# Cross attention and top-2 experts on one core: the norms' last step on ACT, shared weight loads for the scores, one bias product, keys by batch, half of the weight splits on GpSimd

## What is computed

```python
def xattn(query, kv, Wq, bq, Wkv, bkv, Wo, bo):      # 16 heads of 16
    q = query @ Wq + bq
    k, v = split(kv @ Wkv + bkv)
    bias = -slopes[:, None, None] * abs(arange(Nk)[None] - arange(Nq)[:, None] - (Nk - Nq))
    scores = einsum("bhqd,bhkd->bhqk", q, k) / sqrt(16) + bias
    return (softmax(scores) @ v) @ Wo + bo
def ffn(x, Wg, bg, W1, b1, W2, b2):                  # 8 experts, hidden 1024
    gate = softmax(x @ Wg + bg); s, idx = top_k(gate, 2); s = s / (sum(s) + 1e-8)
    return sum over the two chosen e of s_e * (gelu(x @ W1[e] + b1[e]) @ W2[e] + b2[e])
x = x + xattn(layernorm(x), ctx_1024, ...)
x = x + ffn(layernorm(x), ...)
```

## Time and profile before

| | us |
|---|---|
| median of 3 runs | 503.34 |
| lowest, highest | 501.44, 504.68 |
| profiled execution | 508.91 |
| its span | 507.1 |
| busy in the span: PE, DVE, ACT, POOL | 419.6, 312.6, 232.4, 223.7 |
| mean granted clock of PE | 0.922 |

### The profile page before, as it was taken

One profiled execution on the slowest core, in us unless ns is written; L12 is line 12 of the kernel. 1 busy time (PEld: TensorE's weight loads), 2 busy tenths in 40 slices (PEclk: granted clock), 3 DMA queues, 4 the chain that ended last, 5 costly groups with the idle time before them and its releaser, 6 DMA issues. The chain is left out here.

```text
span 507.1 us, 16158 instructions
## 1 busy us (share of the span) xinstructions
PE 419.6 (83%) x5137; PEld 330.3 (65%) x5138; DVE 312.6 (62%) x875; ACT 232.4 (46%) x607; POOL 223.7 (44%) x305
## 2 busy tenths in 40 slices
PE   5565768897888999995179899989989998999981
PEld 2554556676666778873168677668867876777760
DVE  5357848796778777554526466636664765566560
ACT  1333636564555564563234444534543553445430
POOL 3123528887888886677602222222222232122232
PEclk9865979898989999998579999989998999999997
DMA  6574455555646535333322223113222322122110
GB/s 225 134 229 150 139 152 189 175 175 192 215 136 185 165 123 163 122 123 127 127 64 37 39 41 53 35 29 45 46 44 31 53 38 43 34 43 47 22 12 0
DMA packets 52967, 50.70 MB, mean 100 GB/s; under 512 B 22672, under 2 KB 47024, under 8 KB 52784
## 3 DMA queue, kind: packets, MB, share of 16 engines
q1 hardware_dynamic: 45192, 41.07, 27.0%
q0 software_dynamic: 7152, 8.47, 9.9%
q10 hardware_dynamic: 576, 0.53, 0.3%
HBM read 33.73 MB, written 17.50 MB: 101 GB/s over the span
## 5 line engine op out<-in xcount | busy, mean ns | idle before, releaser
L976 PE MATMUL ps<-area,wts 128*128 128x128 f16 (+1 forms) x2896 | 197.0, 243 | 0.1
L976 PEld LDWEIGHTS ps<-area,wts 128*128 (+1 forms) x2896 | 157.5, 103 | 41.0 <-issue 2.1
L976 PE MATMUL ps<-wts,area 128*128 x624 | 153.4, 330 | 2.2 <-DVE area L934 1.8
L718 ACT ACTIVATE area<-ps,late 128x128 f32<-128x128 f32 x312 | 89.2, 368 | 115.0 <-PE ps L976 115.0
L932 DVE TENSOR_SCALAR area<-area 128x512 f16<-128x512 f32 x78 | 33.0, 424 | 77.8 <-ACT area L718 77.7
L976 PE MATMUL ps<-area 128*128 128x154 f16 (+2 forms) x928 | 71.0, 236 | 12.0 <-DMA area<-qd 11.1
L976 PEld LDWEIGHTS ps<-area 128*128 128x128 f16 (+1 forms) x928 | 59.8, 107 | 21.2 <-issue 8.1
L595 POOL DMA_INDIRECT out<-o,row_id x20 | 31.6, 1579 | 95.1 <-issue 65.0
L595 POOL DMA_INDIRECT out<-xn,row_id x19 | 30.0, 1579 | 92.4 <-issue 79.8
L804 DVE TENSOR_REDUCE mx<-ps 128x3 f32<-128x462 f32 (+1 forms) x96 | 53.1, 579 | 24.3 <-PE ps L976 23.9
L621 ACT ACTIVATE area<-ps 128x512 f32<-128x512 f32 x80 | 47.3, 595 | 27.7 <-PE ps L976 25.5
(11 more groups left out here) (121 smaller groups left out, 419.1 us busy)
## 6 DMA issues: line engine op xcount, KB each, us to landing
stage<-in_w SPq DMA_DIRECT2D x32, 512.0 KB, 5.0
area<-xlist SPq DMA_DIRECT2D x39, 130.0 KB, 2.0
area<-qd SPq DMA_DIRECT2D x16, 256.0 KB, 2.7
qd<-wts SPq DMA_DIRECT2D x48, 64.0 KB, 1.9
area<-in_x SPq DMA_DIRECT2D x16, 128.0 KB, 2.3
out<-area SPq DMA_DIRECT2D x16, 128.0 KB, 1.8
xlist<-pad_rows SPq DMA_DIRECT2D x11, 130.0 KB, 2.5
area<-in_b SPq DMA_DIRECT2D x1, 1024.0 KB, 5.0
```

The costliest lines, as they stand in the source:

```text
L718: last = nc.scalar.activation(h32[par][:, c * P:(c + 1) * P], h_ps[par][m][:, f * P:(f + 1) * P], ACT.Gelu_apprx_tanh, bias=b1T[:, ds(e * ...
L976: return nc.tensor.matmul(out_, lhsT, rhs, start=start, stop=stop, skip_group_check=skip)
```

## The change

- `normed1` and `normed2` on POOL end with an operation on one column (-mean x rstd, `rs[:, 2]`); the step on 128x256 is an ACT activation with scale and bias read per partition. ACT has that of the second norm first in its turn, and that of the first norm behind exponential 4 (in the first turns behind the query copy).
- Of a turn's two weight units, the second: ACT makes the high half, then scales the staged unit in place (a third pass), and POOL subtracts, one turn later, between the gate weights and the second norm's `pow`. DVE keeps the first unit.
- Scores: heads go in pairs that share one query weight; one product of 314 columns covers both where both lie in one group. Six of sixteen loads and products go away.
- The output bias is one product of two rows instead of two products of one.
- Keys, their splits and their writes to memory are made batch by batch; ACT issues the writes of the bias rows. In turns before 0 the query product stands ahead of the scores, and DVE's `norm1` ahead of its maxima.

```diff
-GROUPS = [(0, 3), (3, 3), (6, 3), (9, 3), (12, 2), (14, 2)]
+GROUPS = [(0, 3), (3, 3), (6, 2), (8, 3), (11, 3), (14, 2)]
 # SP
+            sp.dma_start(a_sb[:, 0:A_ONE], pack_a[:, 0:A_ONE]).then_inc(s.a_in0, 16)
             load_x(0)
-            sp.dma_start(a_sb, pack_a).then_inc(s.a_in, 16)
...
+            for b in range(B):
+                sp.wait_ge(s.k_hi, b + 1)
+                for a in (0, 1):
+                    sp.dma_start(parts[:, a, :, b], k16[:, b, 0]).then_inc(S[f"kd_w{b}"], 16)
+                sp.wait_ge(s.k_lo, b + 1)
+                sp.dma_start(parts[:, 2, :, b], k16[:, b, 1]).then_inc(S[f"kd_w{b}"], 16)
+                if b == 0:
+                    write_q(0)
 # POOL
+            def rstd(t, mv, rs, ready, done, shifted):
+                pool.wait_ge(ready, t + 1)
                 pool.tensor_tensor(rs[:, 1:2], rs[:, 0:1], c32[:, C_HALF:C_HALF + 1], ALU.pow).then_inc(done, 1)
+                pool.wait_ge(done, t + 1)
+                pool.tensor_scalar(rs[:, 2:3], mv[:, 0:1], rs[:, 1:2], -1.0, ALU.mult, ALU.mult).then_inc(shifted, 1)
-                pool.tensor_scalar(xn, xr[:, t % 8, :], mv1[:, 0:1], rs1[:, 1:2], ALU.subtract, ALU.mult).then_inc(s.xn_d, 1)
...
+            def split_w_lo(u):
+                pool.wait_ge(s.w_sc, seconds.index(u) + 1)
+                pool.tensor_tensor(unit_place(u, 1), staged(u), unit_place(u, 0), ALU.subtract).then_inc(S[f"w_lo{u % NSTAGE}"], 1)
...
                 if f1 is not None:
-                    normed1(f1)
+                    rstd(f1, mv1, rs1, s.ve1_d, s.rstd1, s.shift1)
                 if b2 is not None:
                     weights_of(b2, b2 % 2)
+                for u in weight_units(i - 1)[1:2]:
+                    split_w_lo(u)
                 if b1 is not None:
-                    normed2(b1)
+                    rstd(b1, mv2, rs2, s.ve2_d, s.rstd2, s.shift2)
 # ACT
                 nc.scalar.activation(unit_place(u, 0), staged(u), ACT.Copy, scale=SW).then_inc(s.w_hi, 1)
+                if u in seconds:
+                    act.wait_ge(s.w_hi, u + 1)
+                    nc.scalar.activation(stage[:, u % NSTAGE, :], stage[:, u % NSTAGE, :], ACT.Copy, scale=SW).then_inc(s.w_sc, 1)
...
+                if b2 is not None:
+                    normed2(b2)
                 if f2 is not None and f2 > 0:
-                    normed(f2)
+                    turned(f2)
...
+                if i < -1 and f1 is not None and f1 > 0:
+                    normed1(f1)
...
                     exps(mt, 3)
                     exps(mt, 4)
+                if i >= -1 and f1 is not None:
+                    normed1(f1)
                 for u in units[1:2]:
                     split_w_hi(u)
...
+            def normed2(t):
+                act.wait_ge(s.shift2, t + 1)
+                wait(act, s.x2T_ps, t)
+                wait(act, s.xs_lo, t)
+                nc.scalar.activation(xn2[:], xr[:, t % 8, :], ACT.Identity, bias=rs2[:, 2:3], scale=rs2[:, 1:2]).then_inc(s.xn2_d, 1)
+                act.wait_ge(s.xn2_d, t + 1)
 # DVE
-                for u in earlier[1:2]:
-                    split_w_lo(u)
                 if sc is not None:
                     maxima(sc, 4)
-                for u in units[0:1]:
+                for u in units[0:1] if i < NT else []:
                     split_w_lo(u)
 # PE
+            def keys_of(b):
...
+            keys_of(0)
             pe.wait_ge(s.c_in, 16)
             turn_normed(0)
             pe.wait_ge(s.wq_in, 16)
             query(0)
+            keys_of(1)
...
-                for j in range(n):
-                    hh, p = (first + j) // NP, (first + j) % NP
-                    dst = ps[:, seq % 3, j * KW:j * KW + NK]
-                    last = mm(dst, qs[:, slot, p, :], kk[:, b, p, hh * KW:hh * KW + NK], True, kink is None, True)
+                while at_ < end:
+                    p, hh = at_ // 2, at_ % 2
+                    both = hh == 0 and at_ + 1 < end
+                    width = KW + NK if both else NK
+                    dst = bank[:, (at_ - first) * KW:(at_ - first) * KW + width]
+                    last = mm(dst, qs[:, slot, p, :], kk[:, b, p, hh * KW:hh * KW + width], True, kink is None, True)
...
                 if f2 is not None and f2 > 0:
                     turn_normed(f2)
+                    if i < 0:
+                        query(f2)
...
-                    for z in range(2):
-                        last = mm(misc[:, D:2 * D], c16[0:1, H_SMALL:H_SMALL + P], bo_hl[:, z, :], False, z == 1)
-                    last.then_inc(s.pr_ps, 1)
+                    mm(misc[:, D:2 * D], c16[0:2, H_SMALL:H_SMALL + P], bo_hl[:], False, True).then_inc(s.pr_ps, 1)
```

More of the change, by code:

```diff
@@ L242, in program @@
         bk16, fold = sb("bk16", [H, 2 * DH], f32), sb("fold", [H, DH + 2], f32)
-        bo_hl = sb("bo_hl", [1, 2, D], f16)
+        bo_hl = sb("bo_hl", [2, D], f16)
         def region(e, half):
@@ L318, in weight_units @@
             return list(range(sum(before), sum(before) + count))
+        seconds = [weight_units(i)[1] for i in range(FIRST, LAST) if len(weight_units(i)) > 1]
         def unit_place(u, lo):
@@ L808, in turn @@
                 f1, f2, sc, mt, b1, b2 = stages(i)
-                units, earlier = weight_units(i), weight_units(i - 1)
+                units = weight_units(i)
                 if b2 is not None and b2 > 0:
                     positions(b2 - 1)
-                if sc is not None:
+                if i < 0 and f1 is not None and f1 > 0:
+                    norm1(f1)
+                if sc is not None and i >= 0:
                     for g in range(3):
@@ L816, in turn @@
                     query_lo(f2)
+                if sc is not None and i < 0:
+                    for g in range(3):
+                        maxima(sc, g)
                 if b1 is not None:
@@ L873, in turn @@
                     dve.transpose(nbT[:, sc % 2, :], nb16[:]).then_inc(s.nbT_d, 1)
+                for u in units[0:1] if i >= NT else []:
+                    split_w_lo(u)
                 if i == -3:
@@ L1036, in scores @@
                 first, n = GROUPS[g]
-                for j in range(n):
-                    hh, p = (first + j) // NP, (first + j) % NP
-                    dst = ps[:, seq % 3, j * KW:j * KW + NK]
-                    last = mm(dst, qs[:, slot, p, :], kk[:, b, p, hh * KW:hh * KW + NK], True, kink is None, True)
+                end, bank = first + n, ps[:, seq % 3, :]
+                at_ = first
+                while at_ < end:
[4 more added lines that the diff above has]
+                    last = mm(dst, qs[:, slot, p, :], kk[:, b, p, hh * KW:hh * KW + width], True, kink is None, True)
                     if kink is not None:
                         keys = kinks[:, kink * N_KEYS:kink * N_KEYS + NK]
-                        for m in ((0, 1), (2,))[hh]:
-                            last = mm(dst, diagonal(p, m), keys, False, m > 0, True)
+                        for h in range(at_, at_ + 1 + both):
+                            dst = bank[:, (h - first) * KW:(h - first) * KW + NK]
+                            for m in ((0, 1), (2,))[h % 2]:
+                                last = mm(dst, diagonal(p, m), keys, False, m > 0, True)
+                    at_ += 1 + both
                 last.then_inc(s.s_ps, 1)
@@ L1095, in turn @@
                         scores(sc, g)
-                if f2 is not None and f2 > 0:
+                if f2 is not None and f2 > 0 and i >= 0:
                     query(f2)
```

162 lines of the change are left out of this document (83 added, 79 removed).

## The result

The changed kernel took 530.65 us (median of 4 runs, 526.82 to 533.89), the kernel before beside it 503.98 (501.44 to 504.68): **1.0536** times as long, 95% interval 1.0451 to 1.0621. Measured again beside other kernels, in experiment e11, it was 1.0488 (1.0434 to 1.0543). The forecast was 511, within 496 to 521: right in sign, far too small in size.

What follows compares the result with a forecast made beforehand. A chain through several engines, closing over GpSimd's queue, was taken to bound the ten attention turns. Turns +9.0, TensorE's clock +3, start −4 and last turns 0 gave +8: 511 us on the median of 503.34, range 496 to 521.

Steps and rivals of the forecast that it cites:

- The bound and the new loop: Ten attention turns: a chain through several engines, largely GpSimd's queue, sets the turn; ACT's norm, `xnT` and query follow it.
- GpSimd's split: Second weight unit's rest on GpSimd, ahead of the second norm's `pow`: 2.24 us with its gap, on the loop.
- The blocked short operation: In split turns one short GpSimd operation waits for VectorE's split of the first unit: 1.04 us.
- The scale for ACT: GpSimd has the second norm's scale ready about 10.8 us after the mark, ACT's copy of `x2T`, in split turns.
- The norm on ACT: Second norm's 128x256 last step on ACT: 0.5 us (0.37 to 0.8), 0.55 with its hand-over.
- From norm to copy of `x2T`: Norm on ACT 0.55 us, then to the query's copy 1.62, that copy 0.38, 0.03 more, one behind the other.
- split turns: Seven of the ten turns, in which a second weight unit is split: 13.47 us each; the other three 11.23.
- The steps' sum: Ten turns, before the clock's own term: 128.0 us in place of 119.0, +9.0.
- The start: Before the ten turns: first scores at 21.8 us, 2.5 earlier, and earlier maxima and queries; −4 us together, from 0 to −6.7.
- Rival C: SyncE's queue delays the queries' landing behind a weight load waiting for GpSimd's split: 518 us, chance 0.13.
- TensorE's clock: Gaps over 3 us ahead of the query bring the lower clock: 5.9 us at most, half taken, +3.
- The last turns: Queue ahead of the last scatter gains a split (+2.24), loses blocking; VectorE's split leaves the turn before: about 0, ±2.

Runs made afterwards that it cites:

- e11: The changed kernel as it is, measured again beside other kernels: 1.0488 of the kernel before.
- e8: Changed kernel plus 20 matmuls for nothing on TensorE ahead of the query product in each of seven split turns: 1.0180 of the kernel before.
- e6: Changed kernel with both norms' last steps on GpSimd and the second unit's split on VectorE again: 0.9961 of the kernel before.
- e1: Changed kernel with GpSimd's split moved behind the second norm's `pow` and shift: 0.9965 of the kernel before.
- e7: Changed kernel with second unit's split on VectorE, no scaling pass, second norm on ACT between `o_sb` and the query's copy: 0.9759 of the kernel before.
- e10: e7 with the query's write on SyncE ahead of the finished rows' store and a later tile's load: 0.9767 of the kernel before.
- e15: Changed kernel plus 10 matmuls for nothing, in place of e8's 20, ahead of the query in each split turn: 1.0304 of the kernel before.
- e14: e8 with the last turns' second units split by VectorE, without scaling pass or GpSimd split there: 1.0125 of the kernel before.
- e16: Kernel before plus 12 matmuls for nothing ahead of the transposes of `xn2` in each of the ten turns: 1.0049 of the kernel before.
- e3: Changed kernel with the second unit's split on VectorE again, without ACT's scaling pass or GpSimd's split: 1.0027 of the kernel before.

## Why the prediction was wrong

**Right, with their sizes.** The bound and the new loop: TensorE's longest wait is for `xnT`, and behind it stands GpSimd's queue. GpSimd's split: forecast 2.24, measured 2.13 on average over 14. The blocked short operation: the shift took 1.31 for 0.27, the 1.04 that was kept, with VectorE's split (L819) running from 155.77, beside it. In each of the ten turns one operation met it so: seven times the shift, at 1.29 to 1.33, three times the copy behind it, at 1.22 for 0.18:

```profile
155.77 1.22 DVE L819 SCALAR_TENSOR_TENSOR wts<-stage,wts 128x1024 f16<-128x1024 f32 x1 [0.15 <-ACT wts L616]
```

By the Trainium skill, SBUF — State Buffer, section Who interferes with whom, the operation that comes second waits out the first; the trace agrees again, for VectorE first and GpSimd second. For the other order the prediction read more out of its rows than they hold: L788, which began at 100.67, became 0.26 longer, though GpSimd's L524 ran on beside it for 1.08. The scale for ACT: forecast 10.8 after the mark, measured 10.6 in the turn from 151.47, whose first part is at the full clock. The norm on ACT: I took 0.5 and it is 0.60; the estimate of 0.59 from ScalarE: Activation LUTs, section What ACT_TABLE_LOAD costs, in the Trainium skill was the better one. From norm to copy of `x2T`: forecast 2.58, measured 2.53 in e8 (167.28 to 169.81) at full clock. Together: split turns of 13.47 forecast, 13.20 in e8; the others 11.23 forecast, 11.20 there. The steps' sum of +9.0 for the ten turns measured **+7.0** with the clock at full (126.0 against 119.0, in which before has its own 12.1 us at the lower level). The start: −4 forecast, −3.8 at the first mark, but this is partly luck, for its working did not hold: the first scores were forecast at 21.8, 2.5 us earlier, and came at 23.23, 1.1 earlier; how the rest of the 3.8 arose is not shown. e6, which has it without the norms and the split, reached the first mark at 65.25, 6.0 earlier, and yet measured 0.9961, whose interval includes no gain: its ten turns were 123.2, so most of it is given back in them. Rival C was right to be a rival, but did not happen: in the changed kernel no wait of TensorE for the queries is in the list of the ten turns. It is the next bound, in e1, e7 and e10.

**The step that failed: "TensorE's clock", +3.** It measured **+11.9** (e8 against the changed kernel, in profiles; for the whole kernel the medians say 10 to 11 us and the ratios, 1.0180 for 1.0488 to 1.0536, 16 to 18). I had the level right, and the gap in part: over 3 us in each split turn was forecast, and three of the seven have it (3.8), the others 2.0 to 2.6. I priced only what stood in the one pair of rows that I took, the query's eight passes, 0.84 us more, and called 5.9 us the most. The seven queries did lose 4.2 us, which is within that: 0.92 in four turns, 0.50 in one. The other 7.7 are what was put at nothing. For a low stretch goes on for 3.4 to 10.2 us, and in the changed kernel everything that TensorE does behind the query is on the loop: the transposes of `xn2`, the logits, the next scores that the maxima and the first norm's statistics wait for. In the turn of 15.75 us `pow` was 1.55 us later in its turn by this, before the query's 0.92 is counted. e1 shows the same from the other side: the split moved off is 7 × 2.13 = 14.9 us, and 17.7 came back although TensorE now waited 7.8 us for queries.

**The second step that failed: "The last turns … About 0, ±2".** They measured +6.7. I followed GpSimd's queue to the last scatter and credited VectorE's relief, and left out two things. One is ACT: the scaling pass had been found hidden in the ten turns, where the scale comes late, and I didn't ask again in the last ones, where it comes early. Pass and split cost 3.5 us there at a like clock (e15 against e14). The other is the clock again, for which no term stood in these turns: 2.4 us (58.0 in the changed kernel, 55.6 in e15).

With the measured terms the account closes: +7.0 +11.9 −3.8 +6.7 −1.6 = +20.2. The prediction called 5.9 the most that the clock could cost; it is half of what the ten turns alone showed, and the time came out above the range.

## What to carry to other kernels

When an edit lengthens a wait of TensorE in a loop, read the granted clock by stretches around the waits of that length that the trace already has (here the one at 67.62, whose stretch of 6.8 us the prediction did not read), and price the whole stretch at the lower level by what of it is on the path, not just the first product. Where such a gap can't be closed, some matmuls for nothing in it can pay (20 a turn, 2 to 3% here), but it has to be tried: in the kernel before it made the ten turns 4.1 us longer (e16). A step moved to another engine goes where that engine is waiting for nothing on the loop; here the same two moves, norm to ACT and split kept off GpSimd's path, make 0.976 in place of 1.05 (e7, e10). And cover found in one stage of a kernel has to be looked up again in each other stage.

## What was not expected of the hardware

A low stretch that began in a gap of 3.8 us lasted 10.2 us (from 161.2); the three that began in the ten turns of the kernel before lasted 3.4 us each, and the one around its gap of 3.64 us 6.8 (from 66.3). Idle time alone does not tell where the clock falls: e15 left four gaps of 2.70 us and was granted 0.99, while e3, whose longest gap in the ten turns is 1.81 us, was granted 0.87, with low stretches such as the second line here. It begins in such a gap of 1.81, and TensorE is busy 9.61 of its 10.20 us:

```profile
143.70:153.60 9.90, 7.83 (x118) 5.54 (x116) 9.27 (x28) 7.09 (x15) 6.50 (x16) 1.00 0.47 142
153.60:163.80 10.20, 9.61 (x63) 7.88 (x64) 5.21 (x17) 5.90 (x14) 4.83 (x7) 0.50 0.61 191
```

In e15 ten matmuls of filler stood right ahead of the remaining gap; what it is in this that keeps the clock up, no run here tells apart. Nor is it a matter of the program alone: the last turns of the changed kernel and of e15 are the same instructions, and had 13.3 and 8.1 us at the lower level.
